# Phasor stage: cosine and sine half products in one instruction, and another order of TensorE's work within a unit

## The chip, the cores and the metric

The kernel runs on one core of a Trainium2 chip. The metric is device time in microseconds (us) of one execution; lower is better. Engines are named as in the profile: PE (TensorE; PEld is its weight load), DVE (VectorE), ACT (ScalarE), POOL (GpSimd), and SP, which issues DMAs. An engine executes its own instructions in order; engines meet through semaphores.

## The reference

The model is four layers over x of 8 x 1024 x 256, each added to its input after a layer norm: a phasor stage (first), a feed-forward "coupling" stage, an attention in the Poincare ball, and the coupling stage again. Only the first is touched. Cut to what matters:

```python
k_real = (x @ Wk).reshape(B, T, H, D)          # T = 1024, H * D = 1024
v = (x @ Wv).reshape(B, T, H, D)
k = exp(1j * k_real * 10.0)
rotors = exp(1j * t * freqs)
def step(v, binder, probe):                    # per channel
    mem = cumsum(v * binder, axis=1)           # over the tokens
    return real(mem * probe) / sqrt(t + 1)
out = g_pos * step(v, rotors, conj(rotors)) + g_assoc * step(v, conj(shift(k)), k)
return out @ Wo
```

In real terms a channel needs four running sums over the tokens: v times cosine and v times sine of the position angle, and the same two with the angle of the previous token's k. Each pair is multiplied by the cosine and sine of the present token and added.

## The kernel before, in words

The function `phase_a` (lines 62 to 699) holds the stage. Tokens are split in even and odd ones, T2 = 512 each ("halves"): a tile of 1024 columns is 512 even tokens, then 512 odd. Channels lie on partitions, 128 at a time: NC = 8 chunks. One chunk c of one batch row b is a **unit**, n = 8 b + c, and the stage has 64 units. The batch rows 1 to 6 are a hardware loop; row 0 and row 7 are written out. Every engine runs its own program over the units, with waits on semaphore counts.

For each unit:

- PE, `project` (L597): the angle u = Wk x into the PSUM tile `pu` (four matmuls of 512 columns, L602), then v = Wv x into `pv`, odd half first (L609). A half of `pv` may be written once DVE has used it in all four products of the unit before (`odd_done`, `even_done`).
- ACT, `front` (L506): rounds u (`rnd`, L510), takes the absolute value of the fraction (L512), and forms the cosine and sine of k (`cos_k` L519, `sin_k` L520).
- DVE, `step` (L382): `odd(i)` and `even(i)` (L390, L397) are the products of `pv` with gate and cosine or sine, one instruction of 512 columns each, i = 0, 1 for the position angle and 2, 3 for k's. Odd products go to the PSUM tile `po`, even ones to `mem_c`, `mem_s` in SBUF. `scan(i)` (L404) is the running sum of a pair. `turn_s` (L428) and `turn_v` (L440) multiply the sine sums by the sines. `fraction(n + 1)` (L350) takes the fraction of the next unit's u between `even(3)` and `scan(2)`; it needs ACT's `rnd`, and ACT's `abs` needs it.
- POOL, `post` (L263): five products and sums of 1024 columns, called P1 (L266), A1 (L269), P2 (L275), A2 (L278), A3 (L281) below; A3 ends the unit (`unit_done`).
- PE, `project_out` (L633), once in each unit beside its projections: a quarter of the token tiles of half a batch row's output product. For c = 4 to 7 it uses chunks 0 to 3 of the same row, for c = 0 to 3 chunks 4 to 7 of the row before. With c = 4 and 5 it has four more matmuls (L646, the fold that corrects the first token). It waits for `unit_done` of the unit before, which binds at c = 0 and c = 4. ACT evicts it (L527).

Once in each batch row, at c = 6, PE transposes the next row's normalised input (`transposes`, L586) in four groups through one PSUM bank `pt`, and ACT evicts each (L504) before the next group may start; ACT does it in the middle of `front`, between `abs` and `cos_k`. The sums, variances and normalisation of the next row lie on ACT at c = 1, 2 and 3 to 5, with POOL's small steps `means` (after unit 1) and `scales` (L253, after unit 2) between. In batch row 0, `correction` adds at c = 2 and 3 the one-time work for the fold: eight pairs of transposes with ACT's evictions, and 32 matmul records into `py` (L629), each time ahead of ACT's `front`.

PE's order within unit n (its `batch`, L651): u(n+1), v(n+1) odd half, v(n+1) even half, transposes at c = 6, `project_out`, correction.

Of the kernel before, what the change touches and what calls it, by code (L numbers as in the profile page):

```python
# [21 lines left out]
P = 128  # L22
# [39 lines left out]
def phase_a(nc, x_in, wk, wv, wo, gate, freqs, x_out):  # L62
# [19 lines left out]
    with Scope(nc, "a") as s:  # L82
# [4 lines left out]
        cos_t = s.sb("cos_t", [P, NC, T])  # L87
        sin_t = s.sb("sin_t", [P, NC, T])
# [12 lines left out]
        sin_k = s.sb("sin_k", [P, 2, 2 * (T2 + 1)])  # L101
        cos_k = s.sb("cos_k", [P, 2, 2 * (T2 + 1)])
        mem_c = s.sb("mem_c", [P, 2, 2, T2])
        mem_s = s.sb("mem_s", [P, 2, T2])
        turn_c = s.sb("turn_c", [P, T])
        turn_s = s.sb("turn_s", [P, 2, T])
        turn_v = s.sb("turn_v", [P, 2, T])
# [38 lines left out]
        even_done = s.sem("even_done")  # L146
        sin_turned = s.sem("sin_turned")
# [34 lines left out]
        with nc.Block() as block:  # L182
# [51 lines left out]
            def _(pool):  # L234
# [28 lines left out]
                def post(n, c, free):  # L263
                    s, o = c % 2, out[:, c, :]
                    pool.wait_ge(scan_done, 4 * n + 1)
# [3 lines left out]
                    nc.gpsimd.tensor_tensor(turn_c[:], turn_c[:], turn_s[:, s, :], ALU.add).then_inc(added, 1)  # L269
                    pool.wait_ge(scan_done, 4 * n + 3)  # L270
# [10 lines left out]
                    nc.gpsimd.tensor_tensor(o, o, turn_v[:, s, :], ALU.add).then_inc(unit_done, 1)  # L281

                def pair_of(s, i):

                    return mem_c[:, s, i // 2, :].unsqueeze(1).broadcast_to([P, 2, T2])
# [51 lines left out]
            def _(dve):  # L337
# [44 lines left out]
                def step(n, c, first, last):  # L382
                    s = c % 2
                    odd_by = (cos_t[:, c, T2:T], sin_t[:, c, T2:T], cos_k[:, s, 0:T2], sin_k[:, s, 0:T2])
                    even_by = (cos_t[:, c, 0:T2], sin_t[:, c, 0:T2], cos_k[:, s, T2:T], sin_k[:, s, T2:T])
# [7 lines left out]
                    def evens(i):  # L393
                        return mem_s[:, i // 2, :] if i % 2 else mem_c[:, s, i // 2, :]

                    def even(i):
                        nc.vector.scalar_tensor_tensor(evens(i), pv[:, 0:T2], gates[:, c, i // 2:i // 2 + 1], even_by[i],  # L397
                                                       ALU.mult, ALU.mult).then_inc(even_done, 1)

                    def scan(i):  # L400
                        dve.wait_ge(odd_done, 4 * n + i + 1)
                        dve.wait_ge(even_done, 4 * n + i + 1)
                        o = po[:, 1, :] if i % 2 else evens(i)
                        nc.vector.tensor_tensor_scan(o, evens(i), po[:, i % 2, :], 0.0, ALU.add, ALU.add).then_inc(scan_done, 1)  # L404
# [6 lines left out]
                    if not isinstance(n, int) or n > 0:  # L411
                        dve.wait_ge(scan_done, 4 * n - 1)
                    odd(0)
                    if not isinstance(n, int) or n > 0:
                        dve.wait_ge(last_turned, n)
                    odd(1)
                    dve.wait_ge(v_psum, 2 * n + 2)
                    even(0)
                    even(1)
                    scan(0)  # L420
                    scan(1)
                    dve.wait_ge(trig_done, n + 1)
                    dve.wait_ge(scan_done, 4 * n + 1)
                    odd(2)
                    if not first:
                        dve.wait_ge(added, 2 * (n - 1))
                    dve.wait_ge(scan_done, 4 * n + 2)
                    nc.vector.tensor_tensor(halves(turn_s[:, s, :]), pair_of_last, halves(sin_t[:, c, :]), ALU.mult).then_inc(sin_turned, 1)  # L428
                    even(2)
                    dve.wait_ge(sin_turned, n + 1)  # L430
                    odd(3)
                    even(3)
                    if not last:
                        fraction(n + 1)
                    scan(2)
                    scan(3)
                    if not first:
                        dve.wait_ge(unit_done, n - 1)
                    dve.wait_ge(scan_done, 4 * n + 4)
                    nc.vector.tensor_tensor(halves(turn_v[:, s, :]), pair_of_last, of_tokens(sin_k[:, s, :]), ALU.mult).then_inc(last_turned, 1)  # L440
# [20 lines left out]
            def _(act):  # L461
# [36 lines left out]
                def transposed(b):  # L498
                    for g in range(2 * KD):
# [4 lines left out]
                        nc.scalar.activation(xnT[:, f, h * 512:(h + 1) * 512], pt[:], ACT.Copy).then_inc(xt_done, 1)  # L504

                def front(n, c, first=False, used=False, nxt=None):  # L506
# [6 lines left out]
                    if nxt is not None:  # L513
                        transposed(nxt)
# [27 lines left out]
                def batch(b, first=False, last=False):  # L542
                    for c in range(NC):
                        if first:
                            correction(c)
                        if not (last and c == NC - 1):
                            front(NC * b + c + 1, (c + 1) % NC, used=c >= 1 or not first,
                                  nxt=b + 1 if c == NC - 2 and not last else None)
                        if c >= HC:
                            project_out(2 * NG * b + c - HC, c - HC)  # L550
                        elif not first:
                            project_out(2 * NG * (b - 1) + NG + c, c)
                        if c == SUMS_AT and not last:
# [31 lines left out]
            def _(pe):  # L585
                def transposes(b):  # L586
                    pe.wait_ge(xn_done, NT * b + NT)
                    for g in range(2 * KD):
                        f, h = g // 2, g % 2
                        if g >= 1 or not isinstance(b, int) or b > 0:  # L590
                            pe.wait_ge(xt_done, 4 * b + g)
                        for j in range(4):
                            t = 4 * h + j
                            i = nc.tensor.transpose(pt[:, j * P:(j + 1) * P], xl[:, t, f * P:(f + 1) * P], ident[:])
                        i.then_inc(xt_psum, 1)

                def project(n, c, first=False):  # L597
# [7 lines left out]
                    for h in (1, 0):  # L605
                        if not first:
                            pe.wait_ge(odd_done if h else even_done, 4 * n)
                        for k in range(KD):
                            i = nc.tensor.matmul(pv[:, h * 512:(h + 1) * 512], wv_sb[:, k, c * P:(c + 1) * P],  # L609
                                                 xnT[:, k, h * 512:(h + 1) * 512], start=k == 0, stop=k == KD - 1)  # L610
                        i.then_inc(v_psum, 1)
# [1386 lines left out]
```

## Time and profile before

| | |
|---|---|
| median of 3 runs | 3320.77 us (3317.46 to 3324.61) |
| the profiled execution's own time | 3321.5 us |
| its span, first to last instruction | 3319.7 us |
| granted TensorE clock, mean | 0.951 |
| phasor stage | from 0 to 1027.8 us of the span |
| PE, DVE, ACT, POOL busy, whole span | 2904.2, 1961.8, 1956.1, 1441.8 us |

A chain or a share of the whole span averages over the four layers, so the stage is read by itself. A row of the timeline is "start, duration, engine, line, operation, output<-inputs, count". Consecutive DVE instructions overlap a little in the records; the time that one takes from the engine is the distance to the start of the next one, called its pitch here. A matmul in f32 leaves two records.

### The profile page before, as it was taken

What the parts mean: (1) busy time and instruction counts of PE and PEld (TensorE: products, weight loads), DVE (VectorE), ACT (ScalarE), POOL (GpSimd) and SP (SyncE); (2) the same over time, 40 slices, a digit from 0 to 9 for tenths busy, and PEclk for the clock granted to TensorE, in tenths of its full rate; (3) what the DMA queues carried; (4) which work ended last, traced back from release to release, by engine and by line L of the source; (5) the groups of instructions that cost most, each with busy time, mean ns of one, the idle gap of its engine ahead of it and who ended that gap; (6) DMA issues with size and microseconds to landing.
All of it is one profiled execution on the core that took longest, in us unless ns stands there. A gap on an engine that the chain in (4) does not pass through costs nothing. (4 is left out here: it accounts for less than half of the span.)

```text
span 3319.7 us, 39119 instructions
## 1 busy us (share of the span) xinstructions
PE 2904.2 (87%) x12161; PEld 1261.4 (38%) x12161; DVE 1961.8 (59%) x2773; ACT 1956.1 (59%) x2546; POOL 1441.8 (43%) x893
## 2 busy tenths in 40 slices
PE   2688888888887999953999999999999999979998
PEld 1355555555554444431323233332323232234443
DVE  7798999999994555554344445353444442145545
ACT  4444444544432444421888888787878889844443
POOL 6578888888883333234232313132323230033322
PEclk8899999999998999976999999999999999989999
DMA  2001000010003021123345544536272727231011
GB/s 76 0 20 32 25 29 22 29 35 25 13 26 96 26 76 51 51 75 66 61 89 90 90 90 70 110 60 119 49 131 31 136 32 134 34 106 67 30 51 64
DMA packets 163999, 200.31 MB, mean 60 GB/s; under 512 B 16504, under 2 KB 118272, under 8 KB 163840
## 3 DMA queue, kind: packets, MB, share of 16 engines
q1 hardware_dynamic: 163840, 198.25, 27.1%
q8 instruction: 92, 1.51, 0.2%
q14 instruction: 67, 0.55, 0.1%
HBM read 139.49 MB, written 58.72 MB: 60 GB/s over the span
## 5 line engine op out<-in xcount | busy, mean ns | idle before, releaser
L1827 ACT ACTIVATE b_pr<-b_ps 128x1024 f32<-128x1024 f32 x1024 | 1002.3, 1025 | 257.1 <-PE b_ps L1924 252.7
L1924 PE MATMUL b_ps<-b_st 128*128 128x512 bf16 x2048 | 591.3, 386 | 72.6 <-DMA b_st<-b_scratch 32.0
L1906 PE MATMUL b_acc<-b_pr,b_vaug 128*32 128x512 f32 x4096 | 548.6, 608 | 0.4 <-ACT b_pr L1827 0.4
L1924 PEld LDWEIGHTS b_ps<-b_st 128*128 128x128 bf16 x2048 | 150.2, 98 | 650.3 <-ACT b_pr L1827 381.2
L1225 PE MATMUL f_po<-f_s,f_w 128*128 128x512 f32 x768 | 361.8, 612 | 27.4 <-DVE f_s L1009 13.7
L609 PE MATMUL a_pv<-a_xnT,a_wv 128*128 128x512 f32 x512 | 274.0, 685 | 100.9 <-DVE a_po L390 100.7
L959 POOL TENSOR_TENSOR f_s<-f_cs,f_s 128x512 f32<-128x512 f32 x96 | 164.9, 1717 | 406.9 <-DVE f_cs L1003 406.9
L1100 ACT ACTIVATE f_h<-f_po,f_b 128x512 f32<-128x512 f32 x192 | 131.9, 687 | 249.3 <-PE f_po L1225 249.3
L602 PE MATMUL a_pu<-a_xnT,a_wk 128*128 128x512 f32 x512 | 240.8, 615 | 34.0 <-DVE a_frac L350 33.3
L1543 POOL TENSOR_TENSOR b_SQ<-b_A 128x1024 f32<-128x1024 f32 x32 | 64.7, 2021 | 468.5 <-DVE b_A L1640 468.5
L1225 PEld LDWEIGHTS f_po<-f_s,f_w 128*128 128x128 f32 x768 | 141.5, 192 | 239.8 <-issue 177.4
L1003 DVE TENSOR_SCALAR f_cs<-f_th,f_sc,f_k 128x512 f32<-128x512 f32 x96 | 53.6, 558 | 299.5 <-ACT f_th L1115 290.8
L648 PE MATMUL a_py<-a_wo,a_out 128*128 128x256 f32 x960 | 226.8, 379 | 0.0
L609 PEld LDWEIGHTS a_pv<-a_xnT,a_wv 128*128 128x128 f32 x512 | 107.9, 219 | 264.4 <-DVE a_po L390 141.1
L648 PEld LDWEIGHTS a_py<-a_wo,a_out 128*128 128x128 f32 x960 | 182.7, 190 | 24.5
L275 POOL TENSOR_TENSOR a_out<-a_mem_c,a_cos_k 128x1024 f32<-128x1024 f32 x64 | 139.6, 2182 | 114.9 <-DVE a_mem_c L404 114.9
L1233 PE MATMUL f_po<-f_h,f_w 128*128 128x512 f32 x384 | 175.1, 599 | 2.1 <-PEq L1216 1.8
L1716 DVE COPY b_osb<-b_acc 128x512 f32<-128x512 f32 x64 | 44.3, 692 | 218.8 <-PE b_acc L1906 211.5
L527 ACT ACTIVATE a_xr<-a_py,a_sm 128x256 f32<-128x256 f32 x120 | 50.3, 470 | 207.8 <-PE a_py L648 207.8
L1906 PEld LDWEIGHTS b_acc<-b_pr,b_vaug 128*32 128x32 f32 x4096 | 81.0, 108 | 220.5 <-issue 208.3
L269 POOL TENSOR_TENSOR a_turn_c<-a_turn_c,a_turn_s 128x1024 f32<-128x1024 f32 x64 | 150.9, 2358 | 12.2 <-POOL a_turn_c L266 6.7
L266 POOL TENSOR_TENSOR a_turn_c<-a_mem_c,a_cos_t 128x1024 f32<-128x1024 f32 x64 | 151.1, 2360 | 10.9 <-ACT a_sin_t L570 9.7
(251 smaller groups left out, 4915.6 us busy)
## 6 DMA issues: line engine op xcount, KB each, us to landing
b_st<-b_scratch SPq DMA_DIRECT2D x512, 128.0 KB, 6.9
b_scratch<-b_parts SPq DMA_DIRECT2D x32, 768.0 KB, 8.2
f_xl<-x SPq DMA_DIRECT2D x16, 1024.0 KB, 5.5
f_xr<-x SPq DMA_DIRECT2D x16, 1024.0 KB, 6.8
a_xl<-in_L_attn_a_x_dram SPq DMA_DIRECT2D x16, 512.0 KB, 4.4
x<-a_xr SPq DMA_DIRECT2D x32, 256.0 KB, 2.2
x<-f_xr SPq DMA_DIRECT2D x8, 1024.0 KB, 4.5
b_xl<-x SPq DMA_DIRECT2D x8, 1024.0 KB, 7.7
```

Of the source, the lines that this page charges most:

```text
L266: nc.gpsimd.tensor_tensor(halves(turn_c[:]), pair_of(s, 0), halves(cos_t[:, c, :]), ALU.mult).then_inc(turned, 1)
L269: nc.gpsimd.tensor_tensor(turn_c[:], turn_c[:], turn_s[:, s, :], ALU.add).then_inc(added, 1)
L275: nc.gpsimd.tensor_tensor(halves(o), pair_of(s, 2), of_tokens(cos_k[:, s, :]), ALU.mult).then_inc(turned, 1)
L602: i = nc.tensor.matmul(pu[:, h * 512:(h + 1) * 512], wk_sb[:, k, c * P:(c + 1) * P], xnT[:, k, h * 512:(h + 1) * 512], start=k == 0, stop= ...
L609: i = nc.tensor.matmul(pv[:, h * 512:(h + 1) * 512], wv_sb[:, k, c * P:(c + 1) * P], xnT[:, k, h * 512:(h + 1) * 512], start=k == 0, stop= ...
L648: i = nc.tensor.matmul(o, out[:, c, t * P:(t + 1) * P], wo_sb[:, c, :], start=False, stop=c == c0 + HC - 1)
L959: nc.gpsimd.tensor_tensor(S[k + 1][:, x, 1, c], cs[:, x, c], S[k][:, x, 0, c], ALU.mult).then_inc(b_done[x], 1)
L1225: q = nc.tensor.matmul(po[:, (at + t) % RING, :], w1_sb[:, f, m * P:(m + 1) * P], S[k][:, x, f, h * HT:(h + 1) * HT], start=f == 0, stop=f ...
L1233: q = nc.tensor.matmul(po[:, (at + h) % RING, :], w2_sb[:, f, :], h1[:, x, f, h * HT:(h + 1) * HT], start=f == 0, stop=f == KD - 1)
L1827: nc.scalar.activation(pr[:, 4 * (blk % 2) + j, :], ps[:, j % 2, :], ACT.Exp, scale=SC).then_inc(S["probs_done"], 1)
L1906: x = nc.tensor.matmul(acc[32 * j:32 * j + 32, h * 512:(h + 1) * 512], vaug[:, kt, c:c + 32], pr[:, 4 * (kt % 2) + j, h * 512:(h + 1) * 51 ...
L1924: x = nc.tensor.matmul(ps[:, j % 2, h * 512:(h + 1) * 512], st[:, g % 2, 1, j, kt * P:(kt + 1) * P], st[:, g % 2, 0, j, h * 512:(h + 1) * ...
```

## The change

The cosine and sine tables become halves of one tile (`trig_t`, `trig_k`), and so do the two sums' inputs (`mem`), so that one DVE instruction of 2 x 512 columns makes the cosine and the sine product of a half. DVE's order in a unit becomes even(0), odd(0), even(1), both scans of the position pair, `turn_s`, `fraction(n+1)`, odd(1), both scans of k's pair, `turn_v`; the sine scan comes before the cosine scan. `turn_s` and `turn_v` have one buffer instead of two. PE's order in unit n becomes v(n+1) even half, `project_out`, correction, v(n+1) odd half, transposes at c = 6, u(n+2). The transposes go alternately through `pt` and `py`, and ACT evicts them after `project_out`.

```diff
@@ DVE step
-                    def odd(i):
-                        nc.vector.scalar_tensor_tensor(po[:, i % 2, :], pv[:, T2:T], gates[:, c, i // 2:i // 2 + 1], odd_by[i],
-                                                       ALU.mult, ALU.mult).then_inc(odd_done, 1)
+                    def even(i):
+                        by = trig_k[:, s, :, T2:T] if i else trig_t[:, c, :, 0:T2]
+                        nc.vector.scalar_tensor_tensor(mem[:, s, i], pv[:, 0:T2].unsqueeze(1).broadcast_to([P, 2, T2]),
+                                                       gates[:, c, i:i + 1], by, ALU.mult, ALU.mult).then_inc(even_done, 1)
...
+                        nc.vector.scalar_tensor_tensor(po[:], pv[:, T2:T].unsqueeze(1).broadcast_to([P, 2, T2]),
+                                                       gates[:, c, i:i + 1], by, ALU.mult, ALU.mult).then_inc(odd_done, 1)
+
+                    def scans(i):
+                        dve.wait_ge(odd_done, 2 * n + i + 1)
+                        dve.wait_ge(even_done, 2 * n + i + 1)
+                        nc.vector.tensor_tensor_scan(po[:, 1, :], mem[:, s, i, 1, :], po[:, 1, :], 0.0, ALU.add, ALU.add).then_inc(sin_scanned, 1)
+                        nc.vector.tensor_tensor_scan(mem[:, s, i, 0, :], mem[:, s, i, 0, :], po[:, 0, :], 0.0, ALU.add, ALU.add).then_inc(scan_done, 1)
...
+                    even(0)
+                    dve.wait_ge(v_psum, 2 * n + 2)
+                    if later:
+                        dve.wait_ge(last_turned, n)
+                        dve.wait_ge(scan_done, 2 * n)
                     odd(0)
...
+                    dve.wait_ge(trig_done, n + 1)
                     even(1)
...
+                    scans(0)
+                    if later:
+                        dve.wait_ge(added, 2 * n - 1)
+                    dve.wait_ge(sin_scanned, 2 * n + 1)
+                    nc.vector.tensor_tensor(halves(turn_s[:]), pair_of_last, halves(sin_t[:, c, :]), ALU.mult).then_inc(sin_turned, 1)
                     if not last:
                         fraction(n + 1)
...
+                    dve.wait_ge(sin_turned, n + 1)
+                    dve.wait_ge(scan_done, 2 * n + 1)
+                    odd(1)
+                    scans(1)
+                    if later:
+                        dve.wait_ge(unit_done, n)
+                    dve.wait_ge(sin_scanned, 2 * n + 2)
+                    nc.vector.tensor_tensor(halves(turn_v[:]), pair_of_last, of_tokens(sin_k[:, s, :]), ALU.mult).then_inc(last_turned, 1)
@@ POOL post: P2 waits for the cosine scan of k's pair
-                    pool.wait_ge(scan_done, 4 * n + 3)
+                    pool.wait_ge(scan_done, 2 * n + 2)
@@ PE transposes
+                        if g >= 2 or later:
+                            pe.wait_ge(xt_done, 4 * b + g - 1)
+                        if g == 1 and later:
+                            pe.wait_ge(wo_done, 2 * NG * (b - 1) + NC - 1 - HC)
+                        bank = py if g % 2 else pt
@@ PE project_v, and batch
+                def project_v(n, c, h, first=False):
+                    if not first:
+                        pe.wait_ge(odd_done if h else even_done, 2 * n)
...
                     for c in range(NC):
-                        if c == NC - 1 and not last:
-                            pe.wait_ge(xt_done, 4 * (b + 1) + 4)
+                        n = NC * b + c
                         if not (last and c == NC - 1):
-                            project(NC * b + c + 1, (c + 1) % NC)
-                        if c == NC - 2 and not last:
-                            transposes(b + 1)
+                            project_v(n + 1, (c + 1) % NC, 0)
...
+                        if not (last and c == NC - 1):
+                            project_v(n + 1, (c + 1) % NC, 1)
+                        if c == NC - 2 and not last:
+                            transposes(b + 1)
+                            pe.wait_ge(xt_done, 4 * (b + 1) + 4)
+                        if not (last and c >= NC - 2):
+                            project_u(n + 2, (c + 2) % NC)
```

## Rows read from the trace of the kernel before

**Rows 1.** Stretches: us, each engine's busy time (records), PEclk, DMA share, GB/s.

```profile
160.00:960.00 800.00, 707.97 (x2236) 423.51 (x2236) 747.12 (x846) 370.72 (x612) 663.90 (x306) 0.96 0.08 26
```

**Rows 2.** Groups by form, DVE, 160 to 860 us: busy, mean ns, idle before.

```profile
L350 DVE SCALAR_TENSOR_TENSOR a_frac<-a_rnd,a_pu 128x1024 f32<-128x1024 f32 x49 | 59.7, 1218 | 37.6 <-ACT a_rnd L510 37.6
```

**Rows 3.** Waits, 160 to 960 us: us in total, times, longest.

```profile
ACT a_rnd L510 <- PE a_pu L602: 89.1, 44, 3.0
...
PE a_pv L609 <- DVE a_po L390: 77.0, 41, 4.8
```

**Rows 4.** Timeline, DVE: one unit, first product to the next unit's.

```profile
532.72 0.75 DVE L390 SCALAR_TENSOR_TENSOR a_po<-a_pv,a_gates,a_cos_t 128x512 f32<-128x512 f32 x1
533.37 0.75 DVE L390 SCALAR_TENSOR_TENSOR a_po<-a_pv,a_gates,a_sin_t 128x512 f32<-128x512 f32 x1
...
541.33 1.22 DVE L350 SCALAR_TENSOR_TENSOR a_frac<-a_rnd,a_pu 128x1024 f32<-128x1024 f32 x1
542.46 1.22 DVE L404 TENSOR_TENSOR_SCAN a_mem_c<-a_mem_c,a_po 128x512 f32<-128x512 f32 x1
543.59 1.21 DVE L404 TENSOR_TENSOR_SCAN a_po<-a_mem_s,a_po 128x512 f32<-128x512 f32 x1
544.90 1.23 DVE L440 TENSOR_TENSOR a_turn_v<-a_po,a_sin_k 128x1024 f32<-128x1024 f32 x1
546.04 0.75 DVE L390 SCALAR_TENSOR_TENSOR a_po<-a_pv,a_gates,a_cos_t 128x512 f32<-128x512 f32 x1
```

**Rows 5.** Timeline, DVE: fractions 2, 3, 4 and 63 (the last).

```profile
102.89 1.22 DVE L350 SCALAR_TENSOR_TENSOR a_frac<-a_rnd,a_pu 128x1024 f32<-128x1024 f32 x1
...
128.92 1.22 DVE L350 SCALAR_TENSOR_TENSOR a_frac<-a_rnd,a_pu 128x1024 f32<-128x1024 f32 x1 [10.28 <-ACT a_rnd L510]
...
156.62 1.22 DVE L350 SCALAR_TENSOR_TENSOR a_frac<-a_rnd,a_pu 128x1024 f32<-128x1024 f32 x1 [14.29 <-ACT a_rnd L510]
...
995.32 1.21 DVE L350 SCALAR_TENSOR_TENSOR a_frac<-a_rnd,a_pu 128x1024 f32<-128x1024 f32 x1
```

**Rows 6.** Timeline, PE, at full clock: v, output product with and without fold, u, transposes.

```profile
498.60 3.70 PE L609 MATMUL a_pv<-a_xnT,a_wv 128*128 128x512 f32 x8 [1.87 <-DVE a_po L390]
...
517.18 0.59 PE L644 MATMUL a_py<-a_xr,a_diag 128*128 128x256 f32 x2
...
523.22 3.60 PE L602 MATMUL a_pu<-a_xnT,a_wk 128*128 128x512 f32 x8
526.65 3.60 PE L609 MATMUL a_pv<-a_xnT,a_wv 128*128 128x512 f32 x8
...
545.73 0.66 PE L594 MATMUL a_pt<-a_ident,a_xl 128*128 128x128 f32 x4 [0.77 <-ACT a_xnT L504]
...
560.09 0.59 PE L644 MATMUL a_py<-a_xr,a_diag 128*128 128x256 f32 x2
...
564.41 1.88 PE L602 MATMUL a_pu<-a_xnT,a_wk 128*128 128x512 f32 x4
```

**Rows 7.** Timeline, PE: a v after an idle stretch, at the lower clock.

```profile
511.94 5.40 PE L609 MATMUL a_pv<-a_xnT,a_wv 128*128 128x512 f32 x8 [1.90 <-DVE a_po L390]
```

**Rows 8.** Timeline, DVE and ACT: from a late fraction to the sine.

```profile
528.00 1.22 DVE L350 SCALAR_TENSOR_TENSOR a_frac<-a_rnd,a_pu 128x1024 f32<-128x1024 f32 x1 [2.13 <-ACT a_rnd L510]
...
531.54 1.04 ACT L520 ACTIVATE a_sin_k<-a_frac 128x1024 f32<-128x1024 f32 x1
```

**Rows 9.** Timeline, POOL: P1 of two units in a row, without idle between, and the long step of scales.

```profile
138.80 1.67 POOL L259 TENSOR_TENSOR a_sm<-a_sm,a_cst 128x8 f32<-128x8 f32 x1
...
512.30 2.37 POOL L266 TENSOR_TENSOR a_turn_c<-a_mem_c,a_cos_t 128x1024 f32<-128x1024 f32 x1
...
524.14 2.36 POOL L266 TENSOR_TENSOR a_turn_c<-a_mem_c,a_cos_t 128x1024 f32<-128x1024 f32 x1
```

**Rows 10.** Timeline, PE, batch row 0: v ahead of the first correction; the fold's product.

```profile
118.04 6.15 PE L609 MATMUL a_pv<-a_xnT,a_wv 128*128 128x512 f32 x8 [6.83 <-DVE a_po L390]
...
147.83 7.07 PE L629 MATMUL a_py<-a_wo,a_out 128*128 128x256 f32 x32
```

More of the change, by code:

```diff
@@ L86, in phase_a @@
         wo_sb = s.sb("wo", [P, NC, D])
-        cos_t = s.sb("cos_t", [P, NC, T])
-        sin_t = s.sb("sin_t", [P, NC, T])
+        trig_t = s.sb("trig_t", [P, NC, 2, T])
+        cos_t, sin_t = (trig_t[:, :, i, :] for i in range(2))
         ident = s.sb("ident", [P, P])
@@ L100, in phase_a @@
         frac = s.sb("frac", [P, T])
[L101 to L104, printed above, removed]
+        trig_k = s.sb("trig_k", [P, 2, 2, 2 * (T2 + 1)])
+        cos_k, sin_k = (trig_k[:, :, i, :] for i in range(2))
+        mem = s.sb("mem", [P, 2, 2, 2, T2])
         turn_c = s.sb("turn_c", [P, T])
-        turn_s = s.sb("turn_s", [P, 2, T])
-        turn_v = s.sb("turn_v", [P, 2, T])
+        turn_s = s.sb("turn_s", [P, T])
+        turn_v = s.sb("turn_v", [P, T])
         kap = s.sb("kap", [P, NC])
@@ L393, in evens @@
[L393 to L404, printed above, removed]
+                    later = not isinstance(n, int) or n > 0
@@ L422, in step @@
[L422 to L430, printed above, removed]
@@ L503, in transposed, with front @@
                         f, h = g // 2, g % 2
-                        nc.scalar.activation(xnT[:, f, h * 512:(h + 1) * 512], pt[:], ACT.Copy).then_inc(xt_done, 1)
-                def front(n, c, first=False, used=False, nxt=None):
+                        bank = py if g % 2 else pt
+                        nc.scalar.activation(xnT[:, f, h * 512:(h + 1) * 512], bank[:], ACT.Copy).then_inc(xt_done, 1)
+                def front(n, c, first=False, used=False):
                     act.wait_ge(u_psum, n + 1)
@@ L546, in batch @@
                         if not (last and c == NC - 1):
-                            front(NC * b + c + 1, (c + 1) % NC, used=c >= 1 or not first,
-                                  nxt=b + 1 if c == NC - 2 and not last else None)
+                            front(NC * b + c + 1, (c + 1) % NC, used=c >= 1 or not first)
                         if c >= HC:
@@ L604, in project @@
                     i.then_inc(u_psum, 1)
[L605 to L611, printed above, removed]
+                def project_v(n, c, h, first=False):
+                    if not first:
+                        pe.wait_ge(odd_done if h else even_done, 2 * n)
+                    for k in range(KD):
+                        i = nc.tensor.matmul(pv[:, h * 512:(h + 1) * 512], wv_sb[:, k, c * P:(c + 1) * P],
+                                             xnT[:, k, h * 512:(h + 1) * 512], start=k == 0, stop=k == KD - 1)
+                    i.then_inc(v_psum, 1)
                 def correction(c):
@@ L666, in batch @@
                             correction(c)
+                        if not (last and c == NC - 1):
+                            project_v(n + 1, (c + 1) % NC, 1)
+                        if c == NC - 2 and not last:
+                            transposes(b + 1)
+                            pe.wait_ge(xt_done, 4 * (b + 1) + 4)
+                        if not (last and c >= NC - 2):
+                            project_u(n + 2, (c + 2) % NC)
                 pe.wait_ge(id_done, 2)
@@ L675, in _ @@
                 pe.wait_ge(w_loaded, N_W)
-                project(0, 0, first=True)
+                project_u(0, 0, first=True)
+                for h in range(2):
+                    project_v(0, 0, h, first=True)
+                project_u(1, 1)
                 pe.wait_ge(setup_p, 12 + NT)
@@ L686, in _ @@
                 pe.wait_ge(frac_done, NC * B)
[L687 to L688 removed]
+                pe.wait_ge(odd_done, 2 * NC * B)
+                pe.wait_ge(even_done, 2 * NC * B)
                 for t in range(NT):
```

42 lines of the change are left out of this document (11 added, 31 removed).

## The prediction

> **What bounds the kernel now.** The change touches the first of four layers, so I read that stage alone, and of it the steady part: fraction(4) starts at 156.62 us and fraction(63) at 995.32 [rows 5], 59 units in 838.7 us, 14.215 us each. First the table of stretches [rows 1]: from 160 to 960 us DVE is busy 747 of 800 us, PE 708, POOL 664, ACT 371. DVE is the fullest, but two others are close, so the order of the waits matters as much as the busy time. Second, one unit on DVE's timeline [rows 4]: from one first product to the next is 13.32 us with no gap but one short one. That is DVE's own pace; 59 such units are 786, so 52.8 us of the 838.7 are DVE waiting, 0.9 us per unit. Third, DVE's groups say on what: 37.6 us before the fraction in 49 units, released by ACT's rounding of u [rows 2]. Last, the waits say what is behind that: ACT's rounding waits for PE's u (89.1 us), while PE itself stands idle before v for DVE's products (77.0 us) [rows 3]. So there is a ring: u(n+1) stands on PE behind v(n) and an output product, v(n) stands behind the last products of unit n-1, and the fraction of u(n+1) stands on DVE in the middle of unit n. DVE's pace is the bound, with the ring adding 0.9 us.
>
> **DVE's own work.** Eight half products become four of 2 x 512 columns. A half product's pitch is 0.65 (533.37 - 532.72) [rows 4], 0.66 in the others of a unit, 5.25 for eight. A merged one isn't in the trace. Nearest is the fraction, the same operation on 1024 columns with a PSUM input, but with constants where the products have a gate per partition: 1.13 (542.46 - 541.33). From below: 1.13 each. From above: no gain at all, 2 x 0.66 = 1.32. Between them, the half products and the fraction share a column rate: 512 columns more at 1.13 / 1024 each (0.565) are 1.22, and if the fraction has some fixed part too, 512 columns cost 0.53 and it is 1.19. I take 1.19, 4.76 for four: 0.5 us less a unit. The rest of the unit: four scans of 1.13 (543.59 - 542.46), fraction 1.13, `turn_s` like the fraction 1.13, `turn_v` 1.14. There is one stall for a result just written: today from the last scan to `turn_v`, 1.31 in place of 1.13 [rows 4]. In the new order `turn_v` reads the sine scan, and the cosine scan lies between, so this 0.18 goes; but the sine scan now comes straight behind odd(1), whose result it reads. It comes back there, at the same price. New unit: 4.76 + 4 x 1.13 + 1.13 + 1.13 + 1.14 + 0.19 = 12.87. Against 13.32 that is 0.45 us, 26.6 us in 59 units (bounds: 1.13 each gives 12.63 and 41; 1.32 gives 13.39, a loss of 4).
>
> A page of the Trainium skill (VectorE: DVE Perf Modes, The TRN2 errata) prices an f32 two-input instruction at (N + 151) / 0.96 ns; the records' lengths agree with it (1.22 us at 1024 columns [rows 4]). If pitch went by that, each merge would save 151 / 0.96 = 157 ns, 0.63 us a unit, and the sum below would be 8 us lower. The pitches say less, and I stay with them.
>
> **Schedule of a new unit.** Times from the start of even(0), from these pitches: odd(0) 1.19, even(1) 2.38 to 3.66 (its record is 1.28: 0.75 and 512 columns more, 0.53), scans until 5.9, `turn_s` 5.8, fraction 7.0 to 8.2, odd(1) 8.1 to 9.4, scans until 11.8, `turn_v` 11.7, next unit 12.87.
>
> PE, at full clock: u or v is 3.43 (526.65 - 523.22), half a v 1.72, the output product 4.32 (564.41 - 560.09), with the fold 6.04 (523.22 - 517.18) [rows 6]. v even starts when even(1) ends, 3.7; output product 5.4 to 9.7; v odd to 11.5; u(n+2) to 14.9. v odd is wanted by odd(0) at 12.87 + 1.19 = 14.1: 2.6 us spare. u(n+2) is wanted, with 1.2 of rounding, by the fraction at 19.8: 3.7 spare. Before, v had to be whole inside the stretch that it now has beside other work. So the ring is open: in a plain unit DVE waits for nothing. What is late next is PE in fold units (13.2 instead of 11.5, spare 0.9), and idle on PE falls from about 2 us before v to 12.87 - 11.2 = 1.7.
>
> ACT: from the fraction's start to the end of the sine it takes 4.58 (531.54 + 1.04 - 528.00) [rows 8], 7.0 to 11.5; even(1) wants it at 15.3. That edit (k's products earlier by two scans) costs nothing while the fraction is on time; a late fraction shifts both alike. ACT's extra work for the next row lies behind the eviction; ACT is busy 371 of 800 us [rows 1], and between the sine and the next fraction it has 8 us, so I cost it at nothing. Without that cover its overrun would come off the spare 3.7 of u first.
>
> POOL: one unit back to back is 11.84 (524.14 - 512.30) [rows 9]. P1 starts at 5.95, A1 ends 10.8, P2 now waits for the last scan, 11.8 (before, for the one before it), and A3 ends at 18.8, 6.0 in the next unit. That fits 12.87 with 1.0 to spare. `scales` has one step of 1.67 [rows 9], and I put 0.5 on its three short ones: 2.2, which is 1.2 more than the spare: A3 ends at 7.3 in unit c = 4. There PE's output product waits for it (`unit_done`), behind that wait stand v odd and u, and this is a fold unit: 7.3 + 6.04 + 1.72 = 15.1 against 14.1, so DVE waits 1.0 us. The single buffers of `turn_s` and `turn_v` are free some 8 and 5.5 us before DVE wants them; the cost is nothing, and if POOL fell 5 us behind it would be a DVE wait of the same size.
>
> Transposes: each group waits for an eviction, 0.77 idle [rows 6]. With two banks the groups overlap, but the second must wait until ACT has evicted the output product, behind the sine at 11.5, so about 12.4, and u stands behind all four: they end at 15.0, u at 18.5 and rounded at 19.8 or a little over. With the fold's delays I put 0.4 us on the fraction, once a row. So 1.4 us a row, 0.18 a unit, stays.
>
> Clock: rows at the lower level: a v that followed 1.90 us of idle took 5.40 instead of 3.43 to 3.70 [rows 7], one after 1.87 didn't [rows 6]; mean grant 0.96 [rows 1]. A loss of 2.0 mostly fits in the spare 2.6; for those that meet a fold unit I allow 0.1 a unit. New pace 12.87 + 0.18 + 0.10 = 13.15, against 14.215: 59 x 1.065 = **62.8 us**.
>
> **Batch row 0.** DVE waits 10.28 and 14.29 us for ACT, which evicts the fold's pieces before its rounding [rows 5]. PE began those pieces only after a whole v, started when odd(3) was done, at the low clock: 6.15 us [rows 10]. Now only v even stands ahead, started at even(1), and u of that unit is already made. Followed through at the low clock, fraction(3) comes at 124.6 instead of 128.92, and with the fold's product of 7.07 [rows 10] behind v even, fraction(4) at 149.5 instead of 156.62: **7 us** less (12 if PE were at the full clock).
>
> **Ends.** From the last fraction to the last unit is 1.2 us longer, since odd(1) now lies behind it; the final products wait for the last odd product, 1.1 us earlier in that unit. Zero.
>
> Sum: 63 + 7 = 70 us, from the profiled execution's own 3321.5 us (span 3319.7 and 1.8 around it): 3251.5. It stands 0.7 above the median shown, so **3251 us**, 2.1% faster.
>
> **Rivals.** (a) The merged instruction saves nothing (1.32 each), the order does its part: 3251 + 59 x 0.52 = 3282. For it: no row shows a two-bank output. Against: the fraction reads two banks at 1.13. (b) The ring isn't opened, only moved: PE at the lower clock too often, or fold units two in a row, so half of the 0.9 us wait stays, and no gain in row 0: 59 x (14.215 - 13.32) = 53, less the first row's: 3321 - 53 = 3268, and with a merged price halfway 3283. (c) Both work better: 1.13 each, no clock loss, 12 in row 0: 3251 - 14 - 6 - 5 = 3226.
>
> (d) The other side, slower: TensorE's clock. PE needs per row 8 x 6.86 + 6 x 4.32 + 2 x 6.04 + 5 for the transposes (four of 0.66, three gaps of 0.77 [rows 6]) = 97.9, 12.2 a unit at 2.4 GHz. In the new order it has an idle stretch of 1.7 us ahead of every v even. If each were followed by a stretch at 1.2 GHz that costs 2.0 us [rows 7] it would be 14.2, break-even; at 3.0 us, 15.2, and 59 x 1.0 less 7 gives 3373. It decides from a mean loss of 2.0 per unit. Against it: today's idle stretches are longer and the mean grant is 0.96 [rows 1]. The Trainium skill (TensorE: Matmul & The Clock Gate, A second HAM failure mode: psum-queue depth-cycling) warns of just this, short idles between groups that keep the clock going up and down; the trace of before agrees only in part.
>
> **Chances.** Forecast 0.66 (its own range 3236 to 3272), (a) 0.10, (b) 0.12, (c) 0.07, (d) 0.05. A change of 0.2% (about 7 us) is what a measurement here tells from none. All but (d) are faster; I take 0.03 off them for a gain smaller than that: faster 0.92, same 0.03, slower 0.05. The range takes in (a) and (b), and (c): 3226 to 3288.
>
> **What would show it.** Merged products with a pitch of 1.19 and 256 of them; a unit on DVE of 12.9 without gap; DVE's wait before the fraction under 0.3 us a unit, most at c = 4 to 7; PE waiting for even products before v, not ACT for u; POOL's P2 waiting for the cosine scan. It would be wrong if DVE's gaps stayed with `pv` or ACT's rounding named, or if PE's mean grant in the stage fell below 0.9.

## The result, and the profile after

The changed kernel takes **3245.53 us** (median of 4 runs, 3239.53 to 3250.24) against 3322.69 for the kernel before (3317.46 to 3325.82). The ratio is 0.9768, 95% interval 0.9747 to 0.9790: 2.3% faster. The forecast was 3251 us, range 3226 to 3288. The profiled execution's own time is 3246.4 us (before 3321.5), its span 3244.6 us.

The stretch that answers to [rows 1] (us, busy time of PE, PEld, DVE, ACT, POOL, granted clock, DMA share, GB/s):

```profile
160.00:960.00 800.00, 733.44 (x2423) 453.15 (x2421) 750.17 (x648) 380.06 (x633) 702.72 (x327) 0.99 0.09 29
```

The stage now ends near 953 instead of 1028 us, so this stretch holds a little of the next stage at its end, and still PE and POOL are both fuller than before; the mean grant rose from 0.96 to 0.99.

The timeline of DVE for one unit, which answers to [rows 4]:

```profile
236.97 1.27 DVE L389 SCALAR_TENSOR_TENSOR a_mem<-a_pv,a_gates,a_trig_t 128x1024 f32<-128x1024 f32 x1
238.16 1.28 DVE L394 SCALAR_TENSOR_TENSOR a_po<-a_pv,a_gates,a_trig_t 128x1024 f32<-128x1024 f32 x1
239.35 1.27 DVE L389 SCALAR_TENSOR_TENSOR a_mem<-a_pv,a_gates,a_trig_k 128x1024 f32<-128x1024 f32 x1
240.54 1.22 DVE L400 TENSOR_TENSOR_SCAN a_po<-a_mem,a_po 128x512 f32<-128x512 f32 x1
241.67 1.19 DVE L401 TENSOR_TENSOR_SCAN a_mem<-a_mem,a_po 128x512 f32<-128x512 f32 x1
242.78 1.20 DVE L420 TENSOR_TENSOR a_turn_s<-a_po,a_trig_t 128x1024 f32<-128x1024 f32 x1
243.90 1.21 DVE L350 SCALAR_TENSOR_TENSOR a_frac<-a_rnd,a_pu 128x1024 f32<-128x1024 f32 x1
245.02 1.28 DVE L394 SCALAR_TENSOR_TENSOR a_po<-a_pv,a_gates,a_trig_k 128x1024 f32<-128x1024 f32 x1
246.34 1.23 DVE L400 TENSOR_TENSOR_SCAN a_po<-a_mem,a_po 128x512 f32<-128x512 f32 x1
247.48 1.19 DVE L401 TENSOR_TENSOR_SCAN a_mem<-a_mem,a_po 128x512 f32<-128x512 f32 x1
248.59 1.20 DVE L430 TENSOR_TENSOR a_turn_v<-a_po,a_trig_k 128x1024 f32<-128x1024 f32 x1
249.71 1.27 DVE L389 SCALAR_TENSOR_TENSOR a_mem<-a_pv,a_gates,a_trig_t 128x1024 f32<-128x1024 f32 x1
```

The distances between starts are what counts: 1.19 for a merged product, 12.74 for the unit (13.32 before). There is no gap, and the stall for a fresh result is where it was expected, behind odd(1): 246.34 - 245.02 = 1.32, which is 0.13 over the product's own 1.19.

Fractions 3, 4 and 63, to be held against [rows 5]:

```profile
119.96 1.22 DVE L350 SCALAR_TENSOR_TENSOR a_frac<-a_rnd,a_pu 128x1024 f32<-128x1024 f32 x1 [3.41 <-ACT a_rnd L501]
...
140.94 1.22 DVE L350 SCALAR_TENSOR_TENSOR a_frac<-a_rnd,a_pu 128x1024 f32<-128x1024 f32 x1 [8.15 <-ACT a_rnd L501]
...
917.84 1.21 DVE L350 SCALAR_TENSOR_TENSOR a_frac<-a_rnd,a_pu 128x1024 f32<-128x1024 f32 x1
```

They split the 75.1 us between the two profiled executions: up to fraction(4) 156.62 - 140.94 = 15.7 us; from there to fraction(63) 838.7 - 776.9 = 61.8 us (13.17 us a unit); all that follows took 2.4 us more than before.

Waits from 160 to 960 us, which answer to [rows 3] (total us, times, longest), and DVE's groups from 160 to 860 us, which answer to [rows 2]:

```profile
ACT a_rnd L503 <- DVE a_frac L350: 184.0, 58, 4.6
ACT a_rnd L501 <- PE a_pu L596: 155.7, 46, 4.7
...
PE a_pv L604 <- DVE a_mem L389: 30.1, 28, 1.3
...
DVE a_po L394 <- PE a_pv L604: 18.7, 8, 3.6
PE a_py L639 <- POOL a_out L281: 16.4, 14, 2.2
```
```profile
L394 DVE SCALAR_TENSOR_TENSOR a_po<-a_pv,a_gates,a_trig_t 128x1024 f32<-128x1024 f32 x53 | 68.1, 1284 | 19.1 <-PE a_pv L604 18.5
...
L350 DVE SCALAR_TENSOR_TENSOR a_frac<-a_rnd,a_pu 128x1024 f32<-128x1024 f32 x53 | 64.1, 1210 | 3.8 <-ACT a_rnd L501 3.8
```

The wait before the fraction went from 37.6 to 3.8 us. In its place stand 18.5 us before odd(0), in few long waits. ACT waits longer for u than before (155.7 us against 89.1), and the 3.8 us left before the fraction show that this costs DVE next to nothing. One of the long waits, on PE, with what POOL did ahead of it, and what it came to on DVE:

```profile
253.42 1.98 PE L604 MATMUL a_pv<-a_xnT,a_wv 128*128 128x512 f32 x4 [1.29 <-DVE a_mem L389]
257.59 1.11 PE L639 MATMUL a_py<-a_xr,a_diag 128*128 128x256 f32 x2 [2.19 <-POOL a_out L281]
258.50 1.91 PE L641 MATMUL a_py<-a_fold,a_xnT 128*128 128x256 f32 x4
260.21 2.33 PE L643 MATMUL a_py<-a_wo,a_out 128*128 128x256 f32 x8
262.38 0.59 PE L639 MATMUL a_py<-a_xr,a_diag 128*128 128x256 f32 x2
...
265.40 1.88 PE L604 MATMUL a_pv<-a_xnT,a_wv 128*128 128x512 f32 x4
```
```profile
243.48 1.66 POOL L259 TENSOR_TENSOR a_sm<-a_sm,a_cst 128x8 f32<-128x8 f32 x1
...
254.98 2.34 POOL L281 TENSOR_TENSOR a_out<-a_out,a_turn_v 128x1024 f32<-128x1024 f32 x1
```
```profile
267.31 1.29 DVE L394 SCALAR_TENSOR_TENSOR a_po<-a_pv,a_gates,a_trig_t 128x1024 f32<-128x1024 f32 x1 [3.60 <-PE a_pv L604]
```

The stretch on PE right behind the wait (columns as in the stretch above):

```profile
257.50:260.50 3.00, 2.91 (x7) 2.38 (x8) 2.96 (x4) 2.46 (x3) 2.84 (x2) 0.53 0.03 8
```

At c = 4 the output product waits 2.19 us for POOL's A3, which `scales` had delayed. Its first half then takes 4.79 us (262.38 - 257.59) where 3.02 is normal: the granted clock from 257.5 to 260.5 us was 0.53, from 262.5 on 1.00. The odd half of v is 3.60 us late for DVE. In two of the six batch rows that have this wait the clock did not fall, and the same wait on PE cost DVE 1.94 and 1.93 us. So of the 3.6 us about 1.9 are the wait itself and 1.7 the lower clock.

### The profile page after: what moved, and what is told of

Read it like the earlier page. It is cut to its first block and busy times, and to the rows that moved or that the text cites. A ratio compares the mean times of both kernels' runs of the same rounds, so it can differ in the third digit from the quotient of the medians.

```text
span 3244.6 us, 38427 instructions
## 1 busy us (share of the span) xinstructions
PE 2857.5 (88%) x12027; PEld 1253.5 (39%) x12161; DVE 1926.9 (59%) x2517; ACT 1951.4 (60%) x2546; POOL 1442.8 (44%) x893
## 5 line engine op out<-in xcount | busy, mean ns | idle before, releaser
L1926 PE MATMUL b_ps<-b_st 128*128 128x512 bf16 x1914 | 561.9, 385 | 92.6 <-DMA b_st<-b_scratch 33.2
L604 PE MATMUL a_pv<-a_xnT,a_wv 128*128 128x512 f32 x512 | 251.0, 614 | 47.1 <-DVE a_mem L389 30.1
L503 ACT ACTIVATE a_rnd<-a_frac 128x1024 f32<-128x1024 f32 x64 | 67.7, 1057 | 196.9 <-DVE a_frac L350 196.9
L501 ACT ACTIVATE a_rnd<-a_pu,a_cst 128x1024 f32<-128x1024 f32 x64 | 71.1, 1110 | 166.2 <-PE a_pu L596 166.2
L275 POOL TENSOR_TENSOR a_out<-a_mem,a_trig_k 128x1024 f32<-128x1024 f32 x64 | 139.6, 2181 | 56.4 <-DVE a_mem L401 56.4
L596 PEld LDWEIGHTS a_pu<-a_xnT,a_wk 128*128 128x128 f32 x512 | 99.4, 196 | 165.3 <-issue 130.0
L266 POOL TENSOR_TENSOR a_turn_c<-a_mem,a_trig_t 128x1024 f32<-128x1024 f32 x64 | 151.5, 2368 | 24.9 <-DVE a_mem L401 15.2
```

The costliest lines, as they stand in the source:

```text
L266: nc.gpsimd.tensor_tensor(halves(turn_c[:]), pair_of(s, 0), halves(cos_t[:, c, :]), ALU.mult).then_inc(turned, 1)
L275: nc.gpsimd.tensor_tensor(halves(o), pair_of(s, 2), of_tokens(cos_k[:, s, :]), ALU.mult).then_inc(turned, 1)
L596: i = nc.tensor.matmul(pu[:, h * 512:(h + 1) * 512], wk_sb[:, k, c * P:(c + 1) * P], xnT[:, k, h * 512:(h + 1) * 512], start=k == 0, stop= ...
L1926: x = nc.tensor.matmul(ps[:, j % 2, h * 512:(h + 1) * 512], st[:, g % 2, 1, j, kt * P:(kt + 1) * P], st[:, g % 2, 0, j, h * 512:(h + 1) * ...
```

## The experiments

The kernel before was run beside every experiment, and each ratio is against those runs. The changed kernel gave 3245.53 us and, beside experiments 3, 6 and 7, 3244.23 us. The others (1, 2, 4, 5, 8, 9 and 10) were measured at other times than the changed kernel; a difference to it of less than about 7 us is not clear of noise by the times alone, and there the distance from fraction(4) to fraction(63) in the traces helps.

**1. DVE's part alone** (PE's old order).

```diff
+                            project_u(n + 1, (c + 1) % NC)
                             project_v(n + 1, (c + 1) % NC, 0)
+                            project_v(n + 1, (c + 1) % NC, 1)
+                        if c == NC - 2 and not last:
+                            transposes(b + 1)
...
-                            project_v(n + 1, (c + 1) % NC, 1)
...
-                            project_u(n + 2, (c + 2) % NC)
```

Lines of this edit that are not shown put the transposes back at their old place with one bank, with ACT's eviction inside `front`, and in batch row 0 the correction ahead of the projections.

> DVE's new step with PE's old order (u(n+1), v(n+1) even and odd half, transposes, output product), one bank for the transposes, ACT evicting them inside front; in batch row 0 the correction goes ahead of the projections, because behind them it could not run. Theory of the ring: DVE's own pace stays 12.74, but u(n+1) stands on PE behind v(n) (waits for odd(1), 9.3 us into unit n-1), an output product and itself; 2.4 (fraction to the end of odd(1)) + 3.4 (v) + 4.3 (output product) + 3.4 (u) + 1.2 (rounding) = 14.8 us a unit, more with the fold. So the DVE part alone is SLOWER than the kernel before, 14.9 to 15.2 a unit in place of 14.2: 3350 to 3385 us, with DVE waiting 2 us before every fraction. Rival, the two parts add up: DVE's part gives its 0.6 us a unit by itself, 3283 to 3290 us.

Measured: 3365.56 us against 3322.37; ratio 1.0129 (1.0112 to 1.0146). Slower, as the ring says. PE, the two halves of one v and the start of the output product:

```profile
525.54 1.88 PE L602 MATMUL a_pv<-a_xnT,a_wv 128*128 128x512 f32 x4
529.37 3.34 PE L602 MATMUL a_pv<-a_xnT,a_wv 128*128 128x512 f32 x4 [1.95 <-DVE a_po L394]
532.50 0.98 PE L637 MATMUL a_py<-a_xr,a_diag 128*128 128x256 f32 x2
```

PE does the even half early and then stands 1.95 us for odd(1), with output product and u queued behind; here it then ran the odd half at the lower clock too (3.34 us where 1.88 is normal). From fraction(4) on, the units take 15.26 us on average, 62 us more than before in the 59 units. That the whole kernel is only 43 us slower comes from batch row 0: with the correction ahead of the projections, fraction(4) starts at 134.45 us, against 156.62 before and 140.94 in the changed kernel. Whether the changed kernel would gain by that order of the correction too was not tried. The shorter work of DVE bought nothing, since odd(1) had been moved behind the fraction.

**2. PE: u behind the output product, v whole, two banks.** DVE as before.

```diff
-                            project(NC * b + c + 1, (c + 1) % NC)
+                            project_v(NC * b + c + 1, (c + 1) % NC)
...
+                        if not (last and c >= NC - 2):
+                            project(NC * b + c + 2, (c + 2) % NC)
```

> The kernel before with PE doing u one unit ahead, behind the output product (v(n+1) odd and even half together, output product, transposes through two banks, u(n+2)); DVE's step and its eight half products as before. Theory of the ring: u is off the path and DVE comes near its old pace of 13.33; at c = 6 the transposes and at c = 4, 5 the fold still delay a fraction, 0.3 us a unit: 13.6 to 13.8 in place of 14.2, 3285 to 3300 us. Rival, the split of v around the output product is what opens the ring: then this one stays within 7 us of the kernel before, with DVE waiting for rounding as there.

Measured: 3323.15 against 3322.37 (0.9998, 0.9988 to 1.0008): nothing, and my theory was careless. Written in a row, PE's orders are v(n+1), product(n), u(n+2) in both kernels; "u one unit ahead" only names the list from another start. What was really tried is the transposes' new place and their two banks, and by themselves these give nothing.

**3. v split around the output product, DVE as before.** Experiment 2 with `project_v(..., (1,))` ahead of `project_out` and `project_v(..., (0,))` behind it.

> The kernel before with only PE's v split around the output product (v odd, output product, v even, u), and the transposes through two banks; DVE's step and its eight half products as before, so that odd(3) frees pv 8.1 us into a unit and even(3) 8.7. Theory: the order of v on PE pays only where DVE frees a half of pv early, as its new order does (even(1) at 3.7). Here there is a ring of v odd 1.7, output product 4.3, v even 1.7 and DVE's even(0) to odd(3) 6.7: 14.6 us a plain unit, 16.3 with the fold, 15.0 on average, 59 x 0.8 slower: 3355 to 3385 us. Rival, the split alone opens the ring: 3260 to 3290 us.

Measured: 3464.34 against 3319.83; ratio 1.0435 (1.0418 to 1.0452). The direction is right, the size isn't (3355 to 3385 expected). Some plain units are 14.86 (14.6 expected), but 22 of the 59 take 16.5 to 16.6, and 21 more than 17. One of PE's waits, and the stretch from 160 to 960 us:

```profile
582.62 2.93 PE L616 MATMUL a_pv<-a_xnT,a_wv 128*128 128x512 f32 x3 [3.40 <-DVE a_po L390]
```
```profile
160.00:960.00 800.00, 647.95 (x1916) 383.65 (x1917) 640.08 (x721) 323.05 (x551) 571.53 (x266) 0.91 0.07 23
```

v odd comes behind 3.40 us of idle and mostly runs at the lower clock (2.93 us for three records; at full clock it is 1.45). The difference of 16.55 and 14.86, 1.7 us, is what a half of v takes longer at that clock, so v odd stands in the ring. The mean grant is 0.91. This is the mechanism of rival (d) of the prediction, the clock, in another kernel.

**4. Products apart**, in the new order.

```diff
-                        nc.vector.scalar_tensor_tensor(mem[:, s, i], pv[:, 0:T2].unsqueeze(1).broadcast_to([P, 2, T2]),
+                        for k in range(2):
+                            nc.vector.scalar_tensor_tensor(mem[:, s, i, k, :], pv[:, 0:T2], gates[:, c, i:i + 1], by[:, k, :],
```

> The changed kernel with each merged product as two instructions of 512 columns again, in the same place of the order. Theory: what merging itself is worth is pitch, 4 x (1.32 - 1.19) = 0.5 us a unit; DVE's pace 13.26 instead of 12.74, of which POOL's greater spare gives a part back at c = 4: 22 to 31 us slower than the changed kernel, 3268 to 3277 us. Rival, merging is worth nothing, all is the order: within 7 us of the changed kernel.

Measured: 3258.99 (0.9809, 0.9793 to 0.9826), 13.5 us above the changed kernel; 22 to 31 expected. The pace is 13.24 (13.26 expected). But the gap at c = 5 is 0.8 instead of 1.9 to 3.6, in all six rows: PE waits 1.3 us for A3 instead of 2.2, and the clock does not fall after it. So the slower DVE loses less to POOL and the clock here. From fraction(4) to fraction(63) the experiment takes 786.3 us: 5.2 over 59 x 13.24; the changed kernel takes 776.9, which is 25.2 over 59 x 12.74. Of the 29.5 us that merging gives DVE, 20 went into waits, and 9.4 were left.

**5. Statistics one unit earlier.**

```diff
-    SUMS_AT, VARS_AT = 1, 2
+    SUMS_AT, VARS_AT = 0, 1
...
-                        pe.wait_ge(xsum_done, 2 * NT)
+                        pe.wait_ge(vsum_done, 2 * NT)
```

> The changed kernel with the next row's sums and variances one unit earlier (at c = 0 and 1 instead of 1 and 2), so that POOL's small steps (scales, 2.2 us) lie behind unit 1 and not behind unit 2, whose successor's end PE awaits at c = 4. Theory: the one long gap a row on DVE (1.95 or 3.6 us before odd(0) at c = 5) comes from POOL's A3 being 2.2 us late for the output product at c = 4, and from the lower clock after that idle; it goes: 14 to 22 us faster than the changed kernel, 3224 to 3232 us. Rival, the gap is the two fold units on PE: then it stays, within 7 us.

Measured: 3238.65 (0.9751, 0.9735 to 0.9768), 6.9 us below the changed kernel, where 14 to 22 were expected. From fraction(4) to fraction(63) it is 765.3 us against 776.9. The gap at c = 5 fell to 1.1 us in each of the six rows. POOL catches up only by the difference of DVE's pace and its own, 0.9 us a unit, and at c = 4 PE still stood 1.36 to 1.40 us for A3; the clock did not fall after that.

**6. The same, and the wait at the stage's end moved.**

```diff
-                pe.wait_ge(odd_done, 2 * NC * B)
-                pe.wait_ge(even_done, 2 * NC * B)
                 for t in range(NT):
+                    if t == 4:
+                        pe.wait_ge(odd_done, 2 * NC * B)
+                        pe.wait_ge(even_done, 2 * NC * B)
```

> The changed kernel with the sums and variances one unit earlier (as in the experiment before) and, at the end of the stage, PE's wait for the last products moved from the head of the final eight tiles to the fifth, the first that lies in pv. Theory: PE stood idle 4.55 us there and then ran 2.3 us longer at the lower clock; the last product of unit 62 on POOL ends 2.5 us before the present start, so 2.5 to 5 us go on top of the 7 of the first edit: 3229 to 3236 us. Rival, POOL's last unit is the end of the chain: no gain over the first edit alone, 3238 us.

Measured: 3229.78 (0.9719, 0.9701 to 0.9736), 14.4 us below the changed kernel run beside it and inside the expectation. The second edit's own part is clearest in the traces: from fraction(63) to the next stage's first DVE instruction it is 38.8 us, against 42.97 in experiment 5, 4.2 less. In the changed kernel PE's first matmul of the final tiles waited for odd(1), and ran at the lower clock; with the edit it waits for POOL instead, and ran at full clock here. The lines are of the two kernels:

```profile
932.25 1.19 PE L694 MATMUL a_py<-a_xr,a_diag 128*128 128x256 f32 x2 [4.55 <-DVE a_po L394]
```
```profile
919.22 0.70 PE L695 MATMUL a_py<-a_xr,a_diag 128*128 128x256 f32 x2 [2.16 <-POOL a_out L281]
```

**7. PE's wait for A3 inside the output product.**

```diff
-                    pe.wait_ge(unit_done, units)
+                    pe.wait_ge(unit_done, units - 1)
...
                         for c in range(c0, c0 + HC):
+                            if c == c0 + HC - 1 and j == 0:
+                                pe.wait_ge(unit_done, units)
```

> The changed kernel with PE's wait for the unit before (POOL's A3) moved inside the output product, from its head to the first matmul that reads that unit's chunk: the diagonal, the fold and three chunks, 6 x 0.43 = 2.6 us, run ahead of it; the statistics stay where they were. Theory: the gap at c = 5 is PE's idle for A3 (2.2 us) and the clock after it; both go: 16 to 24 us faster than the changed kernel, 3221 to 3230 us, no gap over 0.6 us left on DVE. Rival, the two fold units in a row are the cause: within 7 us of the changed kernel.

Measured: 3221.63 against 3244.23 for the changed kernel on the same chip; ratio to before 0.9705 (0.9688 to 0.9721). That is 22.6 us less, where 16 to 24 were expected, and PE has no gap ahead of the output product at c = 4:

```profile
355.84 1.98 PE L604 MATMUL a_pv<-a_xnT,a_wv 128*128 128x512 f32 x4 [1.29 <-DVE a_mem L389]
357.66 0.59 PE L639 MATMUL a_py<-a_xr,a_diag 128*128 128x256 f32 x2
```

From fraction(4) to fraction(63) DVE takes 754.3 us, 2.6 over its own pace, and its longest gap there is 0.32 us. The two fold units in a row are as before, so they are not the cause of the long gap.

**8. Both repairs.**

Experiment 7's and experiment 6's second edit together, statistics where they were.

> The changed kernel with both repairs: PE's wait for the unit before inside the output product, and the wait for the last products at the fifth of the final tiles. Theory: the two are at different places and add up; the end gives 4 to 5.5 us (PE's 2.3 us less idle and 2.3 less at the lower clock): 3215 to 3218 us. Rival, what the end gave in the experiment with early statistics was those statistics: within 2 us of the one with the late unit wait, 3220 to 3223.

Measured: 3218.76 (5 runs, 3218.66 to 3220.43; ratio 0.9689, 0.9676 to 0.9702). Its median is the lowest of all, 3.1% under the kernel before, but only 2.9 us below experiment 7, which was measured at another time; it lies between the two expectations, and the times alone do not separate the two kernels. In the traces fraction(63) to the next stage takes 40.3 us against 43.6 in experiment 7, so the second edit gives 3.3 us. PE still waits 2.15 us for POOL at the end, and its first two tiles then took 5.25 us where 3.45 is normal.

**9. One bank for the transposes**, at their new place.

```diff
-                        bank = py if g % 2 else pt
+                        bank = pt
...
-                        if g >= 2 or later:
-                            pe.wait_ge(xt_done, 4 * b + g - 1)
...
+                        if g >= 1 or not isinstance(b, int) or b > 0:
+                            pe.wait_ge(xt_done, 4 * b + g)
```

> The changed kernel with the transposes through the one bank pt again, each group waiting for the eviction of the one before, at their new place. Theory: the four groups end 2 us later (0.66 and 0.6 us in turn instead of overlapped), u(n+2) stands behind them and the fraction at c = 6 has 0.5 us of gap already: 1.3 to 2 us more a row in seven rows, 9 to 14 us slower than the changed kernel, 3253 to 3258 us. Rival, hidden: within 4 us of it.

Measured: 3277.56 (0.9867, 0.9852 to 0.9883), 32 us above the changed kernel, not 9 to 14. PE, the last group of transposes and u, and the granted clock of u's first 3 us:

```profile
406.82 1.07 PE L585 MATMUL a_pt<-a_ident,a_xl 128*128 128x128 f32 x4 [0.69 <-ACT a_xnT L495]
408.65 6.21 PE L593 MATMUL a_pu<-a_xnT,a_wk 128*128 128x512 f32 x8 [0.76 <-ACT a_xnT L495]
```
```profile
408.60:411.60 3.00, 2.95 (x4) 1.41 (x5) 1.75 (x2) 0.00 (x0) 3.00 (x2) 0.50 0.81 259
```

The groups end 2.6 us later than with two banks (408.65 - 402.76 = 5.9 from the first transpose to u, with two banks 3.3); 2 were expected. What I had left out is the clock: four short groups with 0.7 us of idle between them, and then u at the lower level, 6.21 instead of 3.7. Together the fraction comes 4.2 to 5.7 us late in the six rows of the loop, instead of 0.6. In the first row the same four groups were followed by u at full clock (3.70), and the fraction was 2.6 us late instead of 0.4. So the evictions that a second bank hides are worth 2.2 to 2.6 us a row, and the clock 1.5 to 2.6 more in six rows of seven.

**10. Products apart, with the late wait.**

> The kernel with the late unit wait and the merged products apart again. With PE and POOL out of the way DVE is the only bound, and merging should be worth its whole pitch, 4 x 0.125 = 0.5 us a unit: pace 13.24, 59 x 0.5 = 29.5 less the small gaps that vanish: 26 to 31 us slower than the one with the late unit wait, 3248 to 3253 us. Rival, merging is worth what it showed before, 13 us: 3235 us.

Measured: 3251.41 (0.9786, 0.9771 to 0.9801), 29.8 us above experiment 7, which was measured at another time. From fraction(4) to fraction(63) it takes 781.3 us, at DVE's own pace of 13.24 throughout; experiment 7 takes 754.3. The 27.0 us between them are the full pitch of the merging, 29.5, less the 2.6 us of small waits that experiment 7 still has.

## Why the prediction was right, point by point

- **DVE's own work.** The merged product's pitch was taken as 1.19 and is 1.19; four of them save 0.5 us a unit. The length rule of the Trainium skill (VectorE: DVE Perf Modes, The TRN2 errata) would have given 0.63. It fits the length of the fraction's record (1.22 us), less well those of the half products (0.75, by the rule 0.69) and the merged ones (1.28, by the rule 1.22), and it does not carry over to their pitch. The unit was forecast at 12.87 and is 12.74. About half of the difference is the stall behind odd(1), 0.13 over a pitch of 1.19 and not 0.19; most of the rest is that the multiplications `turn_s` and `turn_v` and the scans ahead of them have a pitch of 1.11 to 1.12, not 1.13. So this term was 34 us, not 26.6.
- **What stays of the waits.** 16.5 us were forecast (0.28 a unit), 25.2 came. The place at c = 4 and the cause, A3 delayed by `scales`, were right: A3 ended 7.6 us into the unit, 7.3 forecast. The size was off: I let v odd come 1.0 us late, it is 1.9, and 3.6 where the clock fell. (My own terms give 7.2 for A3's end, 6.0 and 1.2.) Besides A3, PE began 0.3 us after A3's end, and the shorter unit wants v 0.2 us earlier. My allowance for the clock was spread over all units; it belongs behind this one idle stretch. The wait for transposes was 0.57, forecast 0.4. Experiment 7 leaves 2.6 of the 25.2 us, which shows that A3's wait was behind nearly all of it.
- **The two errors cancel, and that is luck**: 59 units at 13.15 forecast, 13.17 measured; 62.8 and 61.8 us. DVE's own work gave 7.6 us more than forecast and the waits took 8.7 more. Over the whole kernel batch row 0 gave 8.7 us more and the end took 2.4, so the sum of 70 against 75.1 is closer than its terms.
- **The ring.** Right that it opens, but my account of it was half wrong. I put it on PE's order, with v's halves in a longer stretch and, in experiment 2's expectation, u ahead. With v whole that order is the same as before, and experiment 2 gave nothing; experiment 3 shows that splitting v alone makes it worse, experiment 1 that DVE's part alone makes it worse. What opens it is the pair: DVE frees the even half of `pv` at 3.7 us of a unit instead of 8.7, since the even products of k stand third, and only then can PE put an output product between the halves. The two parts are +43 and +145 us by themselves and -76 to -77 together. The +43 is a rough measure of DVE's part: experiment 1 also has the transposes' old place and bank, and the other order in batch row 0.
- **Rival (a)**, merging is worth nothing: no, it is worth 13.5 to 29.8 us, by what else binds. **Rival (b)**, fold units two in a row: experiment 7 keeps them and has no gap over 0.32 us in the steady part. **Rival (d)**, the clock: it did not decide here (grant 0.99), though an idle of 1.29 us stood before many even halves (1.7 forecast). It cost time in experiments 3 and 9.
- **Batch row 0.** 7 forecast, 15.7 measured, more than the 12 allowed for full clock. The mechanism was right: v even ahead of the first correction began when even(1) had ended. The size was off, and the clock is only part of it. v even began at 113.25, 4.8 us before the whole v of the kernel before (118.04), and took 1.82 us at full clock where that took 5.99 at the lower one. So the correction's transposes began at 115.07 instead of 124.03; a fraction(3) at 124.6, as forecast, would put them near 120. Lines of the changed kernel and of the one before:

```profile
113.25 1.98 PE L604 MATMUL a_pv<-a_xnT,a_wv 128*128 128x512 f32 x4
115.07 0.60 PE L617 MATMUL a_py<-a_ident,a_wv 128*128 128x128 f32 x4
```
```profile
124.03 0.60 PE L622 MATMUL a_py<-a_ident,a_wv 128*128 128x128 f32 x4
```

  In experiment 7's profile the same v even ran at the lower clock, behind 3.02 us of idle, and fraction(3) came at 121.67, still 2.9 us ahead of the 124.6 that I had followed through at that clock:

```profile
113.27 3.52 PE L604 MATMUL a_pv<-a_xnT,a_wv 128*128 128x512 f32 x4 [3.02 <-DVE a_mem L389]
```

  From fraction(3) to fraction(4) it is 21.0 us (27.7 before, 24.9 forecast), for the same two reasons: an earlier start, and a v even at full clock ahead of the fold's product. Which step of my walk-through lost the rest is not on record.
- **Ends.** Zero forecast, 2.4 us lost: PE stood idle 4.55 us for odd(1) of the last unit and then began at the lower clock. 2.0 of the 2.4 us lie before the next stage's first DVE instruction. I had counted the start and not what the idle would do to the speed behind it.

## What to carry to other kernels

Ask of an order on one engine which instruction of another engine frees its buffer, and how early that can be made: here both halves of the change cost time alone and paid only together. When the busiest engine gets faster, look for the next one in line (here POOL, at c = 4), and put each wait directly ahead of the instruction that needs it, not at the head of a group (one moved wait was worth 22.6 us, against 76 for the whole change). And price an idle stretch on TensorE with the clock that may follow: 2.2 us of waiting cost DVE 1.9 us when the clock held and 3.6 when it fell.

## What was not expected of the hardware

The length of the idle stretch alone does not tell whether the clock falls. The same wait of 2.2 us at c = 4 was followed by the lower level in four rows of the first profile (gap 3.60, 3.60, 3.57, 3.60 on DVE) and not in two (1.94, 1.93); the second profile of the same kernel had three of each. What PE did ahead was the same in all of them: 1.29 us of idle, a half of v at full clock, then the wait. In experiment 5 the wait was 1.4 us at the same place, and the clock held in all six rows. Four transposes with 0.7 us between them were followed by the lower level in six of seven rows of experiment 9. Which condition decides, these runs don't settle. The DVE pitch of the multiplications `turn_s` and `turn_v` fell from 1.13 or 1.14 to 1.11 or 1.12, with the records' length (1.20 instead of 1.22 us); their inputs now lie in one combined tile, and whether that is the reason was not tried.
